# A decoder layer with a selective scan: decay factors in PSUM, and each state summed by a matmul

## What is computed

```
xr = x @ W_in.T; x_ssm, res = split(xr)               # 512 + 512 channels
x_ssm = silu(causal_conv4(x_ssm) + b_conv)
B = (x_ssm @ W_x.T)[:, 16:];  dt = softplus(x_ssm @ W_dt.T + b_dt);  A = -exp(A_log)
h[t] = exp(dt[t]*A) * h[t-1] + dt[t]*B[t]*x_ssm[t]    # 512 channels x 16 states
y[t] = sum over the 16 states of h[t]  +  D*x_ssm[t]
x  = x + (y * silu(res)) @ W_out.T
x  = x + softmax(mask(Q K^T)) V Wo + bo               # Q from x; K, V from a context of 1601 rows
x  = x + top-2-of-8 experts, silu(x W1) * (x W2) @ W3
```

## Time and profile before

| what | value |
|---|---|
| runs of the kernel, median of 3 | 1309.44 us (1306.83 to 1310.84) |
| span of the profiled execution | 1352.2 us |
| busy: TensorE, VectorE, ScalarE, GpSimd | 71%, 70%, 33%, 54% |
| granted TensorE clock, mean | 0.824 |

### The profile page before, as it was taken

How to read it: one execution, slowest core, us unless ns; L and a number is a source line. 1 busy time by engine, 2 the same in 40 slices (tenths; PEclk the granted TensorE clock), 3 DMA queues, 4 the chain that set the end, 5 groups by cost and what they waited for, 6 DMA issues and landing times. The chain is left out here.

```text
span 1352.2 us, 15599 instructions
## 1 busy us (share of the span) xinstructions
PE 966.2 (71%) x4316; PEld 667.9 (49%) x4317; DVE 945.3 (70%) x1313; ACT 446.0 (33%) x823; POOL 728.5 (54%) x497
## 2 busy tenths in 40 slices
PE   3664554958875777885867886797365999999690
PEld 1222211525552434553434563476254999999580
DVE  4499999898998989899989799242721334344134
ACT  2343433424453334353343342022211222222120
POOL 2376667676556586556687665210274444544405
PEclk8776866979986788988688985898586999999795
DMA  9510002000006000005100003000462323211204
GB/s 325 203 32 0 0 32 93 0 7 7 1 32 216 2 0 12 0 0 204 47 0 13 1 0 126 0 13 16 150 224 59 103 95 103 95 39 39 78 28 128
DMA packets 48948, 85.30 MB, mean 63 GB/s; under 512 B 6292, under 2 KB 38696, under 8 KB 46856
## 3 DMA queue, kind: packets, MB, share of 16 engines
q1 hardware_dynamic: 43032, 65.77, 14.4%
q0 software_dynamic: 5872, 19.02, 4.7%
HBM read 65.64 MB, written 14.55 MB: 59 GB/s over the span
## 5 line engine op out<-in xcount | busy, mean ns | idle before, releaser
L404 POOL TENSOR_TENSOR u<-dtx,b_all 128x512 f32<-128x512 f32 x256 | 433.1, 1704 | 233.5 <-DVE h L655 230.8
L655 DVE TENSOR_TENSOR_SCAN h<-da,u 128x512 f32<-128x512 f32 x256 | 415.2, 1644 | 32.9 <-POOL u L404 20.6
L784 PE MATMUL ysum<-h,ident 128*128 128x512 f32 x256 | 186.0, 817 | 226.1 <-DVE h L642 185.5
L486 ACT ACTIVATE da<-dt_,a_neg 128x512 f32<-128x512 f32 x256 | 177.4, 717 | 142.1 <-DVE h L655 141.8
L784 PEld LDWEIGHTS ysum<-h,ident 128*128 128x128 f32 x256 | 50.6, 236 | 314.9 <-DVE h L642 273.0
L642 DVE TENSOR_TENSOR h<-h 128x512 f32<-128x512 f32 x128 | 168.0, 1313 | 0.0
L1373 DVE TENSOR_TENSOR hid<-act_,ps_u 128x352 f32<-128x352 f32 x78 | 40.5, 521 | 120.2 <-ACT act_ L1227 88.8
L924 PEld LDWEIGHTS pv<-pT,ctx_n 128*128 128x128 f32 (+1 forms) x832 | 106.9, 204 | 12.6 <-issue 9.2
L924 PE MATMUL pv<-pT,ctx_n 128*128 128x128 f32 (+1 forms) x832 | 109.5, 287 | 0.0
L895 PE MATMUL pa<-ctx_t,xnT_a 128*128 128x401 f32 (+1 forms) x256 | 107.4, 555 | 1.4 <-ACT xnT_a L531 1.4
L1509 PE MATMUL ps_y<-w_hi,hidT_hi 128*128 x234 | 71.6, 306 | 13.6 <-issue 10.9
(11 more groups left out here) (224 smaller groups left out, 1890.0 us busy)
## 6 DMA issues: line engine op xcount, KB each, us to landing
b_all<-b_dram SPq DMA_DIRECT2D x16, 1024.0 KB, 4.7
ctx_t<-in_ctxT SPq DMA_DIRECT2D x4, 1601.0 KB
ctx_n<-in_ctx SPq DMA_DIRECT2D x4, 1536.0 KB
ffn_sorted<-yg SPq DMA_DIRECT2D x1, 4992.0 KB, 22.4
ffn_sorted<-y_sb SPq DMA_DIRECT2D x39, 128.0 KB
tok_in<-tok SPq DMA_DIRECT2D x35, 128.0 KB
mask<-in_mask SPq DMA_DIRECT2D x16, 200.1 KB, 2.4
w_raw<-in_w1T SPq DMA_DIRECT2D x4, 704.0 KB
```

The lines of the kernel that those rows point to most:

```text
L404: nc.gpsimd.tensor_tensor(u[:, i % 2, :], dtx[:, j % 2, :], b_all[:, n, :], ALU.mult).then_inc(u_ok, 1)
L486: nc.scalar.activation(da[:, i % DS, :], dt_[:, j % 2, :], ACT.Exp, scale=a_neg[:, j, n:n + 1]).then_inc(da_ok, 1)
L655: nc.vector.tensor_tensor_scan(h[:, i % HS, :], da[:, i % DS, :], u[:, i % 2, :], 0.0, ALU.mult, ALU.add).then_inc(scan_ok, 1)
L784: nc.tensor.matmul(ysum[:], ident[:], h[:, 2 * p % HS, :], start=p % (NST // 2) == 0, stop=(p + 1) % (NST // 2) == 0).then_inc(sum_ok, 1)
```

## The change

- da is no longer an SBUF tensor with four rows but two PSUM banks (da0, da1), DS = 2. The banks pt are given up for them. pT's transposes use pa (shared with the scores); the products that used pt[0] (set_up, the row constants, one dt projection) use pv, and the attention's output product uses pv[:, D:2D].
- add_pair is gone. sum_state sums every row of h by a matmul, 64 per batch, and the scan waits for the sum of 8 steps before.
- The gate's projection for batch b + 1 moves into mamba_in (steps 30 to 39 of batch b): ScalarE copies it to SBUF (res_copy), and after the convolution one piece (silus, step 44) does all eight silus. gate has two batches of rows.
- One table AT, with steps listed per tile; ALONE is gone. The hardware loop is unrolled. The small instructions that only held a wait (take_wait, act_scrap, pool_scrap) are gone.
- Waits are changed to suit the shared banks.

```
-    "tile": (15, 22, 29, 35), "fill": (16, 23, 32, 36), "score": (0, 1, 3, 4), "pick": (2, 3, 5, 6), "max": 6,
-    "exp": 9, "inverse": 9, "p_turn": (9, 10, 11, 13), "p_copy": (11, 12, 14, 16), "av": (11, 13, 15, 16), "av_copy": 18,
-    "res_proj": (6, 7, 8, 8), "res_silu": 14,
-    "dt_proj": (52, 5, 19, 34), "softplus": (57, 9, 25, 39), "dt_add": (58, 10, 26, 40), "dtx": (60, 12, 28, 42),
-    "ln_m_stat": 21, "ln_m_root": 22, "ln_m_norm": 23, "ln_m_turn": 25, "ln_m_copy": 28,
-    "in_proj": (29, 31, 37, 39), "tap": (32, 34, 40, 42), "conv": (33, 35, 41, 43), "conv_silu": 46,
-ALONE = {
...
+    "score": ((15, 16, 17, 18), (19, 20, 22, 23), (28, 29, 30, 31), (37, 38, 39, 40)),
+    "pick": ((17, 18, 19, 20), (21, 22, 24, 25), (30, 31, 32, 33), (39, 40, 41, 42)),
+    "fill": (15, 18, 28, 37), "max": (20, 25, 33, 42), "exp": (23, 28, 36, 45), "inverse": (26, 31, 39, 48),
+    "p_turn": ((24, 25, 26, 27), (32, 33, 34, 36), (41, 42, 43, 44), (46, 47, 48, 49)),
+    "ln_m_stat": 11, "ln_m_root": 12, "ln_m_norm": 13, "ln_m_turn": 13, "ln_m_copy": 16,
+    "in_proj": (17, 22, 24, 27), "tap": (19, 24, 27, 30), "conv": (20, 25, 28, 31),
+    "res_proj": (30, 33, 37, 39), "res_copy": (32, 35, 40, 42), "silu": 44,
+    "b_proj": 46, "b_copy": 49,
+    "dt_proj": (52, 5, 18, 34), "softplus": (56, 9, 21, 37), "dt_add": (57, 10, 22, 38), "dtx": (59, 12, 24, 40),
...
-    DS = 4
-    PAIRS = STEPS // 2
+    DS = 2
...
-        pt = [ps("pt0"), ps("pt1")]
         pv = ps("pv")
+        da = [ps("da0"), ps("da1")]
...
-                def silu_conv(m):
+                def silus(m):
                     act.wait_ge(conv_step, (TAPS - 1) * (m * KI + KI))
                     for j in range(KI):
                         nc.scalar.activation(of_row(xs, m, j), of_row(xs, m, j), ACT.Silu).then_inc(silu_ok, 1)
+                    act.wait_ge(res_ev, m * KI + KI)
+                    for j in range(KI):
+                        nc.scalar.activation(of_row(gate, m, j), of_row(gate, m, j), ACT.Silu).then_inc(res_ok, 1)
                     exp_and_ln()
...
                             wait(act, scan_ok, b * STEPS + i - DS + 1)
-                            nc.scalar.activation(da[:, i % DS, :], dt_[:, j % 2, :], ACT.Exp,
+                            nc.scalar.activation(da[i % DS][:], dt_[:, j % 2, :], ACT.Exp,
...
-                            if i % 2 == 0:
-                                wait(dve, sum_ok, b * PAIRS + i // 2 - HS // 2 + 1)
-                            nc.vector.tensor_tensor_scan(h[:, i % HS, :], da[:, i % DS, :], u[:, i % 2, :], 0.0,
+                            wait(dve, sum_ok, b * STEPS + i - HS + 1)
+                            nc.vector.tensor_tensor_scan(h[:, i % HS, :], da[i % DS][:], u[:, i % 2, :], 0.0,
...
-                def sum_pair(b, p):
-                    if p % (NST // 2) == 0:
-                        wait(pe, y_ok, b * KI + p // (NST // 2))
-                    pe.wait_ge(pair_ok, b * PAIRS + p + 1)
-                    nc.tensor.matmul(ysum[:], ident[:], h[:, 2 * p % HS, :], start=p % (NST // 2) == 0,
-                                     stop=(p + 1) % (NST // 2) == 0).then_inc(sum_ok, 1)
+                def sum_state(b, i):
+                    if i % NST == 0:
+                        wait(pe, y_ok, b * KI + i // NST)
+                    pe.wait_ge(scan_ok, b * STEPS + i + 1)
+                    nc.tensor.matmul(ysum[:], ident[:], h[:, i % HS, :], start=i % NST == 0,
+                                     stop=i % NST == NST - 1).then_inc(sum_ok, 1)
...
-                with pe.Fori(1, B - 1) as b:
+                for b in range(1, B - 1):
                     body(b, True, True, True)
```

More of the change, by code:

```diff
@@ L388, in body @@
                 def body(b, scan, inp, att_):
-                    when = AT if scan else ALONE
+                    when = AT
                     a, m = b - 1, b + 1
@@ L505, in body @@
                                     act.wait_ge(ip_mm, m * KI + k + 1)
-                                    nc.scalar.copy(act_scrap[:, k:k + 1], ident[:, 0:1])
                                     nc.scalar.activation(of_row(xs, m, k), CONV_BANKS[k][:], ACT.Identity, bias=b_conv[:, k:k + 1],
                                                          scale=w_conv[:, k, TAPS - 1:TAPS]).then_inc(tap_ok, 1)
-                            if i == when["conv_silu"]:
-                                silu_conv(m)
+                            for k in range(KI):
+                                if i == when["res_copy"][k]:
+                                    act.wait_ge(res_mm, m * KI + k + 1)
+                                    if att_ and k == 0:
+                                        act.wait_ge(yg_ok, b * KI)
+                                    nc.scalar.copy(of_row(gate, m, k), RES_BANKS[k][:]).then_inc(res_ev, 1)
+                            if i == when["silu"]:
+                                silus(m)
                             if i == when["b_copy"]:
@@ L562, in _ @@
                 body(0, True, True, False)
-                with act.Fori(1, B - 1) as b:
+                for b in range(1, B - 1):
                     body(b, True, True, True)
@@ L688, in body @@
                                     convolve(m, k)
-                            if not scan and i == when["conv_silu"]:
+                            if not scan and i == when["silu"]:
                                 set_up_biases()
@@ L736, in _ @@
                 body(0, True, True, False)
-                with dve.Fori(1, B - 1) as b:
+                for b in range(1, B - 1):
                     body(b, True, True, True)
@@ L884, in attention @@
                     for q in range(T):
-                        s = i - when["tile"][q]
-                        if s in when["score"]:
-                            c = when["score"].index(s)
+                        if i in when["score"][q]:
+                            c = when["score"][q].index(i)
                             lo, hi = CHUNKS[c]
@@ L904, in attention @@
+                        if i in when["av"][q]:
+                            g = when["av"][q].index(i)
+                            if q > 0 and g == 0:
+                                pe.wait_ge(x2_ok, a * T + q)
                             elif g == 0:
                                 pe.wait_ge(c_ok, a + 1)
-                            elif scan:
-                                pe.wait_ge(res_ok, b * KI + 3)
-                            for c in range(4 * g, min(4 * g + 4, KC)):
-                                w = P if c < KC - 1 else S2_LAST
-                                last = nc.tensor.transpose(pt[g % 2][0:w, (c - 4 * g) * P:(c - 4 * g + 1) * P],
-                                                           sim[:, q % 2, c * P:c * P + w], ident[:])
@@ L912, in attention @@
-                            last.then_inc(pt_mm, 1)
-                        if s in when["av"]:
-                            g = when["av"].index(s)
-                            if q > 0 and g == 0:
-                                pe.wait_ge(av_ok, a * T + q)
-                            elif scan and g == 0:
-                                pe.wait_ge(res_ok, b * KI + KI)
                             pe.wait_ge(pt_ok, NPT * (a * T + q) + g + 1)
@@ L950, in body @@
                 def body(b, scan, inp, att_):
-                    when = AT if scan else ALONE
+                    when = AT
                     for i in range(STEPS):
                         if att_ and i == 0:
-                            sum_pair(b - 1, PAIRS - 1)
-                        if scan and i >= 2 and i % 2 == 0:
-                            sum_pair(b, i // 2 - 1)
+                            sum_state(b - 1, STEPS - 1)
+                        if scan and i >= 1:
+                            sum_state(b, i - 1)
                         if att_:
```

205 lines of the change are left out of this document (89 added, 116 removed).

## The result

The changed kernel takes 1218.71 us (median of 4 runs, 1217.78 to 1219.2) against 1310.14 (1306.83 to 1311.11) for the kernel before on the same chip: ratio 0.9299, interval 0.9283 to 0.9315, 91 us less. Forecast were 1180 and a range of 1130 to 1275. The profiled execution has a span of 1216.0 us.

A forecast was written before the change was run, and what follows sets the result against it. TensorE was to replace VectorE as the bound in batches 1 to 3. Profiled: 63 + 118 + 189 + 186 + 156 + 104 + 406 = 1222 us against 1352.2; less the profiled execution's extra, 1180, range 1130 to 1275.

The forecast's parts named there:

- VectorE: Scan batches: without pair additions and with scans at 1.25 us, VectorE's work is 101, 143, 131 and 101 us.
- E: Rival for the scan: from PSUM it still takes 1.64 us, meeting GpSimd as before; about 1206 us, chance 0.03.
- TensorE's work: Scan batches: with 64 sums per batch instead of 32, TensorE has 95, 174, 171 and 141 us.
- Start and end: First scan at 63 us instead of 54.1; attention alone at the end 104 us instead of 99.9.
- The DMA queue: Loads of b_all's quarters from step 52 on stay hidden, costed at nothing; otherwise under 10 us a batch.
- The profiled execution's extra: Whole span: the profiled 1352.2 us exceeds the 1309.44 median by 3.2%; taken off as a fixed extra, giving 1179.
- "How full can the bound be?": Scan batches: TensorE 92% busy gives 189, 186 and 156 us for batches 1 to 3; batch 0 takes 118.
- the prediction's own signs of being right: Scans 1.2 to 1.3 us, products near 1.27, TensorE about 90% busy, clock over 0.92, batches 1 and 2 under 195.
- Rival B: Scan batches: coupling, no engine binds and the bound engine is 82% busy; about 1263 us, chance 0.2.
- A: The forecast itself: TensorE binds at a warm clock; 1180 us, own range 1140 to 1225, chance 0.62.
- Batch 0: No attention: two-scan loop 84 us, VectorE's work 101, 4.5 us standstill for ScalarE's silus; 118 us instead of 175.
- C: Scan stretches: short pauses keep TensorE's clock low; at 0.70 the kernel takes about 1388 us, chance 0.07.

The follow-up runs named there:

- e12: The kernel before the change, unedited, profiled once more: span 1310.3 us, its run 1312.18 us.
- e6: Changed kernel with all of ScalarE's table work one step later relative to da: 1194.82 us.
- e8: Changed kernel with VectorE reading the bank ysum out one step earlier after each quarter: 1183.63 us.
- e7: Changed kernel with each sum entering TensorE's queue two steps behind its scan instead of one: 1172.25 us.
- e1: Changed kernel with 15 of each 16 sums cut to 256 of 512 columns, every wait kept (y incomplete): 1191.85 us.
- e10: Changed kernel with sums and ScalarE's table work one step later, ysum read one step earlier, and 15 of 16 sums cut to 256 columns: 1152.64 us.
- e2: Changed kernel with da back in SBUF, still two rows deep, and h with 6 rows instead of 8: 1320.55 us.
- e3: Changed kernel with four da rows, two in PSUM and two in SBUF, and h with 6 rows instead of 8: 1261.38 us.

## Why the prediction was right, and where it was off

**VectorE, right.** Forecast 101, 143, 131 and 101 us for batches 0 to 3, measured 98, 129, 129 and 114. The scan was taken at 1.25 us and has a median of 1.223. Batch 3's is 13 too low, batch 1's 14 too high, for the windows of the earlier trace rows gave 7 scans too many to batch 1 and 8 too few to batch 3. The same working with the batches cut at their first scans gives 132 and 115. Neither binds. E is out: no scan over 1.225 us.

**TensorE's work, right.** Forecast 95, 174, 171 and 141, measured 101, 176, 173 and 146: 15 us too low over all four, at a clock of 0.90 to 0.95 where some 0.95 was expected.

**Start and end, right within 8 us.** The first scan came at 55.7, not 63: the first silus began 3 us later than before (34.04 against 31.07) instead of 9, so the gate's projections lie almost entirely under the convolution. The tail took 102.4 us against 104. The DMA queue costs nothing that shows: the scan's waits name ScalarE, GpSimd and, for 5.3 us, TensorE, and GpSimd's products wait for no load. The unrolled loops were not taken by themselves.

**The profiled execution's extra, right.** Taking 43 us off as something outside the change was right, and e12 shows where it lay.

**"How full can the bound be?", the step that failed.** Forecast was TensorE at 92% in the full batches, and 118 us for batch 0. Measured are 86, 87 and 89%, and 132.3 us for batch 0 (77%). The scan stretches were 649 us by forecast and 697.6 in the trace: 49 too short. Of this some 17 us come from TensorE's work (595.8 against 581, at the forecast's own 581/649 busy), the rest, 32, from how full it is. With start and tail (9 us the other way) that is the 40 us between 816 and 855.7 at the first expert load, and 1180 against 1218.71. Of the prediction's own signs of being right, the durations of scans and products came; scans of batches 1 and 2 under 195 us (203 and 198), TensorE busy about 90% in every scan stretch and a clock over 0.92 in all of them did not.

The reasoning that VectorE, as the bound, was busy 91 to 93% in a program coupled alike, and that TensorE would keep 92%, was the mistake. VectorE bound alone: TensorE had 25% of slack or more, GpSimd and ScalarE mostly waited for VectorE. TensorE now stands inside the loop with work of its own in nearly every step: its queue takes a sum one step after the scan, and the scan in turn waits for work that stands behind that sum. This contrast is argued from the waits; that the hand-overs cost time is shown by e6 to e8. Rival B named this, and its price of 82% (1263) was as far off on the other side; the truth lies between A and B. With one hand-over loosened, in e7, the batches come near the forecast's numbers: 125, 187, 185 and 153 us against 118, 189, 186 and 156, and 1172.25 us against 1180. That doesn't show its mechanism. A says that TensorE's work sets the time; yet taking some 110 us of it off gave 27 us in the changed kernel (e1) and 22 with all three hand-overs moved (e10). That TensorE's work and a margin come near what the loops allow is partly luck.

**Batch 0** was forecast by the loop over two scans (84 us of 64 steps) with 4.5 us per burst of ScalarE. What it missed: ScalarE waits for TensorE's projections with da behind them. The burst itself was priced nearly right: silus and two table loads ran from 324.36 to 331.23 us in batch 1, and VectorE stood still 5.24 us before the next scan, against 4.5 forecast:

```profile
324.36 1.28 ACT L431 ACT_TABLE_LOAD   x1
325.65 2.19 ACT L431 ACTIVATE xs<-xs 128x512 f32<-128x512 f32 x4
327.75 2.17 ACT L434 ACTIVATE gate<-gate 128x512 f32<-128x512 f32 x4
329.94 1.28 ACT L411 ACT_TABLE_LOAD   x1
331.71 0.70 ACT L450 ACTIVATE da<-dt_,a_neg 128x512 f32<-128x512 f32 x1
...
332.44 1.22 DVE L611 TENSOR_TENSOR_SCAN h<-da,u 128x512 f32<-128x512 f32 x1 [5.24 <-ACT da L450]
```

**Rival E was priced wrong,** though it didn't happen: 26 us were given for scans of 1.64 us, since VectorE's work still lay under TensorE's. e2 is that case, with GpSimd's products longer as well, and costs 102. An engine's total below the bound's total doesn't make a longer instruction free when it is in the loop.

**C,** the low clock, did not come true as a whole (0.91 for the execution, 0.90 to 0.95 in the batches). e1 and e10 show that its mechanism is there: the clock falls when TensorE gets less to do between the same waits.

## What to carry to other kernels

Before moving work from the bound engine to the next one, draw the loops that the hand-written order closes through the new bound engine's queue, and give each hand-over a second step of slack: here the same sums one step later were worth 46 of 1219 us, half as much as the change itself. Two such moves can cancel each other, as e7's and e8's do where the sum and its read-out meet in one step. A contended instruction inside such a loop can cost about as much as it gets longer (102 us for 102 in e2, 43 for 55 in e3) even where its engine is idle a quarter of the time, and work taken off a TensorE that waits is partly given back as a lower clock. Check a part of the program that the change does not touch in both traces before reading the difference of their spans, and count an instruction that each stage has equally often before calling a window a stage.

## What the runs showed of the hardware that was not expected

- A scan of 128x512 float32 with one operand in PSUM is as fast as the best SBUF form: 1.190 us minimum in both, median 1.223. The price of 0.04 to 0.08 us that L615 suggested doesn't carry over.
- ScalarE's exponential into PSUM takes 0.691 us (median), into SBUF 0.722 in e2 for the same shape.
- Cutting some 110 us of TensorE's columns lowered its busy time by 63 us and the granted clock of batch 0 from 0.91 to 0.77.
- One profiled execution was 3.2% longer than the runs beside it, all of it in one phase, with the busy time of every engine but TensorE unchanged.
